# Swapping the rope halves with two DMAs instead of four, and the last layer norm moved from GpSimd to ScalarE

## The chip, the cores and the metric

The kernel runs on one core of a Trainium2 chip. The metric is the device time of one execution in microseconds (us), as the median over several executions. A core has TensorE (PE) for matmuls, VectorE (DVE), ScalarE (ACT) and GpSimd (POOL) for elementwise work, and SyncE (SP), which here only issues DMAs. Each engine runs its own instructions in order; engines wait for each other through semaphores.

## The reference

The reference is one decoder layer with a layer norm after each part, on x of 64 x 64 tokens with 256 columns:

```
x = layernorm(x + self_attention(x))          # 16 heads of 128, causal, ALiBi
x = layernorm(x + cross_attention(x, ctx))    # latent keys, 16 heads, q_rope and k_rope of 64
x = layernorm(x + ffn(x))                     # ternary weights, activations rounded to 8 bits
```

The change touches the rope of the cross-attention and the last layer norm:

```
def _rope(x, L):
    half = x.shape[-1] // 2
    ...
    x1, x2 = (x[..., :half], x[..., half:])
    return jnp.concatenate([x1 * cos - x2 * sin, x1 * sin + x2 * cos], axis=-1)

def _layernorm(x, axis=-1, eps=1e-05):
    m = jnp.mean(x, axis=axis, keepdims=True)
    v = jnp.var(x, axis=axis, keepdims=True)
    return (x - m) / jnp.sqrt(v + eps)
```

## The kernel before

The residual stream `X` stays on chip as 32 blocks of 128 tokens by 256 columns. Three parts follow each other: self-attention, cross-attention, feed-forward. Each engine's program is written out by hand, and each part is a software pipeline: in slot n an engine works on items n, n-1, n-3 and so on, in the order in which the code lists them. Values are often split into two bf16 halves, a high and a low part, and multiplied in three passes.

**Cross-attention loop.** 64 steps, 8 token tiles of 512 tokens times 8 pairs of heads. In step n:

- PE: scores of item n-3 (L914, L921), the rope part `ropeP` and the latent part `latP` of the queries of item n (L931), the weighted sum `oP` of item n-5 (L939), a transpose `ptP` of item n-4 (L947), the projection of item n-7 (L958).
- ACT: eight exponentials of item n-3 (L973), `pth` of n-4 (L980), two copies of `latP` into `qh` (L985), `oA` of item n-5 (L992).
- DVE: the reciprocal (L1013), `ptl` (L1018), the row maxima `ntop` (L1023), `turn` (L1027), then `qh` of item n-1 (two instructions, L1036), then the cosine product (L1041), once per eight steps the accumulation into `X` (L1048), in four of eight steps statistics of a block (L543).
- POOL: the normalisation of the probabilities (L1063), `oBl` (L1068), and `qhl`, the low part of `qh` (L1075), which waits for `qh`.
- SP: four DMAs `oB<-oA` for item n-6 (L893), then four DMAs `x_turned<-x_turn` for item n (L901).

The rope works on 128 partitions, two heads of 64 rows. DVE multiplies the rope part by sine (`turn`), SP's DMAs bring each row to the partition of its partner in the other half (`turned`), and one step later DVE adds the turned rows to the cosine product. The two halves of a head lie in 32 consecutive partitions each, so a swap takes four DMAs of 32 rows. The queue goes in order: the swap of item n is issued after the four DMAs of item n-6. `turn` and `turned` have two buffers.

**Feed-forward loop.** 32 blocks. In slot n: PE gate and up products of block n (`gP`, `uP`, L1211), the down product `dP` of block n-3 (L1219), transposes `hmP` of block n-2 (L1226). ACT: `sig` of block n (L1237), `ds` of block n-3 (L1243, from `dP`), `hqT` of block n-2 (L1248). DVE: `hs` of block n (L1298), its maximum (L1301), three small instructions (L1303 to L1306), then mean and variance of block n-3 (L1310, L1312), which wait for `X`. POOL: the add of `ds` to `X` for block n-3 (L1266), `hm` of block n (L1270), after every fourth block the roots of four blocks (L1257, L1259), and the normalisation of block n-7 (L1200). DVE normalises the last four blocks at the end, and SP stores four blocks with one DMA (L1288).

Of the kernel before, what the change touches and what calls it, by code (L numbers as in the profile page):

```python
# [11 lines left out]
P = 128  # L12
# [568 lines left out]
def cross_weights(a, sem, sb):  # L581


    x_stage = sb("x_stage", [P, 2, CC, TILE], F32)
    okv = sb("okv", [P, H * (C + 2 * KVC)], F32)
    wo = okv[:, 0:H * C].rearrange("p (h n) -> p h n", h=H)
    ukT = okv[:, H * C:H * (C + KVC)].rearrange("p (h n) -> p h n", h=H)
    uvT = okv[:, H * (C + KVC):].rearrange("p (h n) -> p h n", h=H)
    uqT = sb("uqT", [P, H, QC], F32)
    qr = sb("qr", [QC, H * R], F32)  # L590
    dqf, kvf, wkr = sb("dqf", [P, CC, QC], F32), sb("kvf", [P, CC, KVC], F32), sb("wkr", [KVC, 2 * R], F32)
    tabs = sb("tabs", [P, 3, T], F32)
# [7 lines left out]
    loads = [(keys[:, :], a["keys"], s_seg), (seg[0:T, :], a["segT"], s_seg), (seg[T:P, :], a["segT"], s_seg),  # L600
             (dqf[:, :, :], by_rows("L0_xattn_W_dq"), s_w), (kvf[:, :, :], by_rows("L0_xattn_W_kvc"), s_w),
             (wkr[:, :], a["wkr"], s_w), (tabs[:, :, :], a["rope"].rearrange("p (k t) -> p k t", k=3), s_w),
             (uqT[:, :, :], by_rows("uqT"), s_w), (ukT, by_rows("ukT"), s_w), (uvT, by_rows("uvT"), s_w),
             (wo, by_rows("L0_xattn_W_o"), s_w), (qr[:, :], a["L0_xattn_W_qr"], s_w)]
    return {"x_stage": x_stage, "s_ctx": [sem("l_ctx0"), sem("l_ctx1")], "okv": okv, "wo": wo, "ukT": ukT, "uvT": uvT, "uqT": uqT, "qr": qr, "dqf": dqf, "kvf": kvf, "wkr": wkr,
            "tabs": tabs, "mask": mask, "square": square, "s_mask": sem("l_mask"), "seg": seg, "segf": segf, "keys": keys, "loads": loads,
            "s_weights": s_w, "weights": 9 * 16, "s_seg": s_seg, "s_segf": sem("l_segf"), "s_square": sem("l_square"), "s_ffn": sem("l_ffn"), "s_abs": sem("l_abs"), "w_sums": sb("w_sums", [P, 3], F32)}
# [226 lines left out]
def cross_attention(nc, a, X, norm, next_norm, ident, late, sem, sb, part):  # L834
# [42 lines left out]
    with nc.Block() as block:  # L877
        @block.sync
        def _(sp):
            def ffn_weights(k, name):  # L880
                cols = CC * DFF
                src = a[name].rearrange("(c p) n -> p c n", p=P)
                dst = late["okv"][:, k * cols:(k + 1) * cols].rearrange("p (c n) -> p c n", n=src.shape[2])
                sp.dma_start(dst, src).then_inc(late["s_ffn"], 16)

            for n in range(N + PROJ_AT):
                m = n - PV_AT - 1
                if has(n, PV_AT + 1):
                    wait(sp, s_oe, m + 1)
                    wait(sp, s_proj, m - 1)  # L890
                    for par in range(2):
                        for i in range(2):
                            sp.dma_start(oB[i * KVC:(i + 1) * KVC, m % 2, par * HT:(par + 1) * HT],  # L893
                                         oA[par * KVC:(par + 1) * KVC, m % 2, i, :]).then_inc(s_ot[m % 2], 16)
                if has(n, 0):
                    wait(sp, s_turn, n + 1)
                    wait(sp, s_qh, n - 1)
                    half = R // 2
                    for r in range(0, P, half):
                        o = r + half if r % R == 0 else r - half  # L900
                        sp.dma_start(turned[o:o + half, n % 2, :], turn[r:r + half, n % 2, :]).then_inc(s_swap[n % 2], 16)  # L901
                if 8 <= n < 11:
                    ffn_weights(n - 8, ("wgT", "wuT", "wdT")[n - 8])

# [99 lines left out]
        def _(dve):  # L1004
# [3 lines left out]
            for n in range(N + PROJ_AT):  # L1008
# [14 lines left out]
                    nc.vector.tensor_reduce(ntop[:, :], by_token(sP[:, :]), AX, ALU.max, negate=True).then_inc(s_top, 1)  # L1023
                if has(n, 0):
                    wait(dve, s_ropeP, n + 1)
                    wait(dve, s_swap[n % 2], 64 * (n // 2))
                    nc.vector.tensor_tensor(by_token(turn[:, n % 2]), by_token(ropeP[n % 2][:, :]), tabs[:, 1, :].unsqueeze(1).to_broadcast([P, BT, T]),  # L1027
                                            ALU.mult).then_inc(s_turn, 1)
                if has(n, 1):
                    m = n - 1  # L1030
                    wait(dve, s_swap[m % 2], 64 * (m // 2 + 1))
                    wait(dve, s_cos, m + 1)
                    wait(dve, s_s, m - 2)
                    for i in range(2):
# [43 lines left out]
def feed_forward(nc, a, X, norm, eps_col, ident, late, out, sem, sb, part):  # L1078
# [105 lines left out]
        "sig", "h", "max", "sc", "inv", "dsc", "hm", "te", "ds", "y"))  # L1184
    s_stats, s_mom, s_rstd, s_normed, s_out = (sem("f_" + n) for n in ("stats", "mom", "rstd", "normed", "out"))
    GROUP = 4
    NG = NB // GROUP
    moments = sb("ln3_moments", [P, NB, 2], F32)
    rstd, power = sb("ln3_rstd", [P, NB], F32), sb("ln3_power", [P, GROUP], F32)
    s_eps, s_power = sem("f_eps"), sem("f_power")  # L1190

    def blocks(slot, lags):

        for n in range(NB + lags):
            slot(n, lambda lag: 0 <= n - lag < NB)

    def normalise(eng, i):

        x = X[:, i, :]
        return eng.tensor_scalar(x, x, moments[:, i, 0:1], rstd[:, i:i + 1], ALU.subtract, ALU.mult)  # L1200

    with nc.Block() as block:  # L1202
        @block.tensor
        def _(pe):
            def slot(n, has):
# [8 lines left out]
                if has(3):  # L1214
                    e = n - 3
                    wait(pe, s_te, e + 1)
                    wait(pe, s_ds, e - 1)
                    for f in range(FC):
                        last = nc.tensor.matmul(dP[e % 2][:, 0:C], hqT[:, e % 2, f * P:(f + 1) * P], wd[:, f, :], start=(f == 0), stop=(f == FC - 1))  # L1219
                    last.then_inc(s_dn, 1)  # L1220
# [11 lines left out]
        def _(act):  # L1232
            def slot(n, has):
                if has(0):
                    wait(act, s_g, n + 1)
                    wait(act, s_h, n - 1)
                    nc.scalar.activation(sig[:, n % 2, :], gP[:, :], ACT.Sigmoid, scale=gsc[:, n:n + 1]).then_inc(s_sig, 1)  # L1237
                if has(3):
                    e = n - 3
                    wait(act, s_dn, e + 1)  # L1240
                    wait(act, s_dsc, e + 1)
# [8 lines left out]
            blocks(slot, 3)  # L1250

        @block.gpsimd
        def _(pool):
            def roots(m):
                own = slice(m * GROUP, (m + 1) * GROUP)
                wait(pool, s_mom, (m + 1) * GROUP)
                nc.gpsimd.tensor_scalar(rstd[:, own], moments[:, own, 1], EPS, None, ALU.add).then_inc(s_eps, 1)  # L1257
                wait(pool, s_eps, m + 1)
                nc.gpsimd.tensor_tensor(rstd[:, own], rstd[:, own], power[:, :], ALU.pow).then_inc(s_rstd, 1)  # L1259

            def slot(n, has):
                if has(3):
                    e = n - 3
                    wait(pool, s_ds, e + 1)
                    x = X[:, e, :]
# [5 lines left out]
                if has(4) and (n - 4) % GROUP == GROUP - 1:  # L1271
                    roots((n - 4) // GROUP)
                if has(7) and n - 7 < NB - GROUP:
                    e = n - 7
                    wait(pool, s_rstd, e // GROUP + 1)
                    normalise(nc.gpsimd, e).then_inc(s_normed, 1)

            nc.gpsimd.memset(power[:, :], -0.5).then_inc(s_power, 1)
            pool.wait_ge(s_power, 1)
            blocks(slot, 4)  # L1280

        @block.sync
        def _(sp):
            dst = out.rearrange("(n p) c -> p n c", p=P)
            for m in range(NG):
                own = slice(m * GROUP, (m + 1) * GROUP)
                sp.wait_ge(s_normed, (m + 1) * GROUP)
                sp.dma_start(dst[:, own, :], X[:, own, :]).then_inc(s_out, 16)  # L1288
            sp.wait_ge(s_out, 16 * NG)

        @block.vector
        def _(dve):
            def slot(n, has):
# [12 lines left out]
                    nc.vector.tensor_scalar(dsc[:, n:n + 1], hsc[:, n:n + 1], wsc[:, 2:3], None, ALU.mult).then_inc(s_dsc, 1)  # L1306
                if has(3):
                    e = n - 3
                    wait(dve, s_y, e + 1)
                    nc.vector.bn_stats(stats[:, e, :], X[:, e, :]).then_inc(s_stats, 1)  # L1310
                    wait(dve, s_stats, e + 1)
                    nc.vector.bn_aggr(moments[:, e, :], stats[:, e, :]).then_inc(s_mom, 1)  # L1312

            blocks(slot, 3)
            dve.wait_ge(s_rstd, NG)
            for i in range(NB - GROUP, NB):
                normalise(nc.vector, i).then_inc(s_normed, 1)


def constants():  # L1320
# [7 lines left out]
    freq = 1.0 / 10000.0 ** (np.arange(half) / half)  # L1328
    ang = (np.arange(T)[:, None] * freq).T
    cos, sin = np.concatenate([np.cos(ang)] * 2), np.concatenate([-np.sin(ang), np.sin(ang)])  # L1330
    rope = np.concatenate([np.tile(cos * SCALE, (2, 1)), np.tile(-sin * SCALE, (2, 1)), np.concatenate([cos, sin])], axis=1)
    keys = np.tile(np.arange(T) + LOOKBACK / 2, (P, 1))
    return {"ident": np.eye(P, dtype=np.float32), "bias": bias.astype(np.float32),
# [34 lines left out]
```

## Time and profile before

| | |
|---|---|
| median of 3 executions | 1605.5 us (1603.73 to 1607.73) |
| profiled execution, whole / its span | 1607.42 us / 1605.6 us |
| mean granted clock of TensorE | 0.965 of full speed |
| busy in the span | PE 1426.0, ACT 1251.4, POOL 1226.7, DVE 1224.6 us |
| DMA issues `x_turned<-x_turn` | 256, of 64 KB each |
| DMA issues `oB<-oA` | 256, of 64 KB each |
| DMA issues `out<-X` | 8, of 512 KB each |

Times are from the start of the span. A row of the timeline has the start, the duration, the engine, the line and what is written from what, then in brackets the idle time of the engine before it and what ended it. Idle time of an engine that does not bound the kernel costs nothing. SPq is SP's DMA queue; its durations are issue times, and the time to landing is listed apart.

### The profile page before, as it was taken

Reading aid. Unit: us, or ns where it says so; the run is one execution under the profiler, and the core shown is the slowest. Engines: PE = TensorE matmul, PEld = TensorE weight load, DVE = VectorE, ACT = ScalarE, POOL = GpSimd, SP = SyncE. Lnnn points to the kernel's source line nnn. Section 1 sums busy time; section 2 is a strip of 40 time slices with the busy share of each in tenths; the row PEclk is TensorE's granted clock in tenths of the full one; section 3 lists DMA queues with packets and bytes.
Section 4 is the critical chain, followed back from the end, with each engine's and each line's share of the span. In section 5 each row is a group of like instructions: output and inputs, shape, how many; then the busy total and the mean of one; then the engine's idle time right before and its main releaser. Section 6 shows DMA issues by size and latency. Waiting matters only on the chain. (4 is left out here: it accounts for less than half of the span.)

```text
span 1605.6 us, 54080 instructions
## 1 busy us (share of the span) xinstructions
PE 1426.0 (89%) x19943; PEld 1060.9 (66%) x20146; DVE 1224.6 (76%) x2873; ACT 1251.4 (78%) x3981; POOL 1226.7 (76%) x1146
## 2 busy tenths in 40 slices
PE   5988999999999999999999987868889898846996
PEld 3666777777777777777777764435666666634664
DVE  3877777777777777777777787876777778747986
ACT  5877888888888888888888874667878888856664
POOL 5899889888888988888898864546667767711787
PEclk9999999999999999999999987999999999976998
DMA  6600000000000000000000001026334444310011
GB/s 225 184 3 16 16 3 16 16 2 16 16 15 3 16 16 2 16 16 3 16 16 2 3 2 54 27 58 171 95 93 99 96 97 101 94 28 0 14 40 53
DMA packets 59763, 70.64 MB, mean 44 GB/s; under 512 B 16464, under 2 KB 44432, under 8 KB 59504
## 3 DMA queue, kind: packets, MB, share of 16 engines
q1 hardware_dynamic: 59504, 67.18, 15.5%
q8 instruction: 163, 2.67, 0.7%
q14 instruction: 96, 0.79, 0.2%
HBM read 29.39 MB, written 4.19 MB: 21 GB/s over the span
## 5 line engine op out<-in xcount | busy, mean ns | idle before, releaser
L420 DVE SCALAR_TENSOR_TENSOR X<-projP,r,X 128x256 f32<-128x256 f32 x512 | 211.3, 476 | 3.7 <-PE projP L254 3.6
L1075 POOL TENSOR_TENSOR qhl<-qh 128x1024 bf16<-128x1024 f32 x64 | 121.2, 1893 | 108.5 <-issue 67.5
L234 PEld LDWEIGHTS svP<-W,xT 128*128 128x128 bf16 x3072 | 182.6, 98 | 30.5 <-issue 0.6
L973 ACT ACTIVATE x_probs<-xsP,x_ntop 128x64 f32<-128x64 f32 x512 | 152.5, 328 | 58.1 <-DVE x_ntop L1023 57.7
L480 POOL TENSOR_TENSOR y_sql<-y_sq 128x512 bf16<-128x512 f32 x128 | 133.0, 1039 | 80.8 <-ACT y_sq L321 80.4
L234 PE MATMUL svP<-W,xT 128*128 128x128 bf16 x3072 | 192.7, 219 | 0.0
L205 PE MATMUL qkssP<-xT,W 128*128 128x512 bf16 x641 | 161.8, 383 | 33.7 <-issue 20.3
L205 PE MATMUL kP<-xT,W 128*128 128x512 bf16 x768 | 188.8, 382 | 0.0
L254 PE MATMUL projP<-W,y 128*128 128x256 bf16 x1024 | 178.9, 277 | 3.3 <-POOL yl L480 3.2
L336 ACT ACTIVATE probs<-scores,ntop 128x64 f32<-128x64 f32 x512 | 170.4, 339 | 1.4 <-DVE ntop L410 1.4
L480 POOL TENSOR_TENSOR k_sql<-k_sq 128x512 bf16<-128x512 f32 x128 | 133.1, 1040 | 21.5 <-ACT k_sq L341 20.9
L254 PE MATMUL projP<-W,yl 128*128 128x256 bf16 x512 | 141.7, 277 | 0.0
L1036 DVE TENSOR_TENSOR qh<-xropeP,x_turned 64x512 f32<-64x512 f32 x128 | 88.3, 689 | 69.2 <-DMA x_turned<-x_turn 67.8
L515 POOL TENSOR_TENSOR ql<-q 128x512 bf16<-128x512 f32 x128 | 139.4, 1089 | 0.0
L480 POOL TENSOR_TENSOR q_sql<-q_sq 128x512 bf16<-128x512 f32 x128 | 133.0, 1039 | 6.9 <-ACT q_sq L328 6.9
L205 PEld LDWEIGHTS kP<-xT,W 128*128 128x128 bf16 x768 | 75.7, 99 | 92.5 <-issue 3.3
L518 POOL TENSOR_TENSOR vl<-v 128x512 bf16<-128x512 f32 x128 | 135.4, 1058 | 0.0
L480 POOL TENSOR_TENSOR yl<-y 128x512 bf16<-128x512 f32 x128 | 133.0, 1039 | 0.0
L450 DVE TENSOR_TENSOR ptl<-pyP,pth 128x256 bf16<-128x256 f32 x128 | 54.3, 424 | 96.8 <-ACT pth L355 96.8
L433 DVE COPY v<-svP 128x512 f32<-128x512 f32 x128 | 88.4, 691 | 42.8 <-PE svP L234 41.9
L205 PEld LDWEIGHTS qkssP<-xT,W 128*128 128x128 bf16 x768 | 65.0, 98 | 82.0 <-issue 13.0
L407 DVE SCALAR_TENSOR_TENSOR scores<-svP,r,bias 128x64 f32<-128x64 f32 x512 | 110.0, 278 | 4.5
(197 smaller groups left out, 4768.1 us busy)
## 6 DMA issues: line engine op xcount, KB each, us to landing
x_turned<-x_turn SPq DMA_DIRECT2D x256, 64.0 KB, 2.0
oB<-oA SPq DMA_DIRECT2D x256, 64.0 KB, 2.1
w_stage<-in_wqkvp SPq DMA_DIRECT2D x16, 512.0 KB, 3.3
x_stage<-in_xT SPq DMA_DIRECT2D x8, 512.0 KB, 4.1
X<-in_x SPq DMA_DIRECT2D x1, 4096.0 KB, 17.0
x_stage<-in_ctxT SPq DMA_DIRECT2D x8, 512.0 KB, 3.7
out<-X SPq DMA_DIRECT2D x8, 512.0 KB, 2.9
okv<-in_L_xattn_W_o SPq DMA_DIRECT2D x1, 2048.0 KB, 11.8
```

The lines of the kernel that those rows point to most:

```text
L205: last = nc.tensor.matmul(dst[:, :], weight(parity, u, i, c), xT[:, z, c, tok], start=(c == 0 and k == 0), stop=(c == CC - 1 and k == 2))
L234: last = nc.tensor.matmul(svP[:, b * D:(b + 1) * D], xT[:, u, c, t * TILE + b * P:t * TILE + (b + 1) * P], weight(parity, z, 2, c), start= ...
L254: last = nc.tensor.matmul(projP[:, b * C:(b + 1) * C], y_part, W[:, (j - 3) // NT % 2, z, 3 * CC * D:], start=(i == 0), stop=(i == 2))
L336: last = nc.scalar.activation(probs[:, b, :], scores[:, b, :], ACT.Exp, bias=ntop[:, b:b + 1], accum_out=total[:, b:b + 1])
L407: last = nc.vector.scalar_tensor_tensor(scores[:, b, :], svP[:, b * T:(b + 1) * T], r[:, b:b + 1], row, ALU.mult, ALU.add)
L420: last = nc.vector.scalar_tensor_tensor(acc, projP[:, b * C:(b + 1) * C], r[:, PB + b:PB + b + 1], acc, ALU.mult, ALU.add)
L433: nc.vector.tensor_copy(v[:, j % 4, :], svP[:, :]).then_inc(s_ve, 1)
L480: return nc.gpsimd.tensor_tensor(dst[:, :], src[:, :], high(src, slice(None), 0, TILE), ALU.subtract)
L515: nc.gpsimd.tensor_tensor(ql[:, j % 2, :], q[:, j % 2, :], high_of(q, j % 2), ALU.subtract).then_inc(s_ql, 1)
L518: nc.gpsimd.tensor_tensor(vl[:, j % 4, :], v[:, j % 4, :], high_of(v, j % 4), ALU.subtract).then_inc(s_vl, 1)
L973: last = nc.scalar.activation(probs[:, m % 2, b % PB, b // PB, :], sP[:, b * T:(b + 1) * T], ACT.Exp, bias=ntop[:, b:b + 1], accum_out=tot ...
L1075: nc.gpsimd.tensor_tensor(qhl[:, m % 3, :], flat, flat.bitcast(BF16)[:, 1::2], ALU.subtract).then_inc(s_ql, 1)
```

## The change

Two independent edits.

*Rope.* The columns of `W_qr` and of both parts of `wkr`, and the rows of the cosine and sine tables, are permuted on the host so that row i of the first half and row i of the second lie in neighbouring partitions, 2i and 2i+1. The partner of every row is now its neighbour. Two DMAs of 64 rows, each every second partition, swap them: even rows to odd ones and odd rows to even ones. The semaphore of a swap counts 32 instead of 64.

*Last layer norm.* In the loop, ACT normalises blocks 0 to 27, eight slots after the block entered, as `rstd * x + shift`, after `hqT`. POOL no longer normalises; it computes `shift = -mean * rstd` for each group of four with two more small instructions. The last four blocks form groups of three and one. For the last three blocks (29 to 31), DVE computes the add to `X` straight from `dP`, in place of `ds` on ACT and the add on POOL. The last stores are of three blocks and of one.

```
-                    half = R // 2
-                    for r in range(0, P, half):
-                        o = r + half if r % R == 0 else r - half
-                        sp.dma_start(turned[o:o + half, n % 2, :], turn[r:r + half, n % 2, :]).then_inc(s_swap[n % 2], 16)
+                    for h in range(2):
+                        sp.dma_start(turned[1 - h::2, n % 2, :], turn[h::2, n % 2, :]).then_inc(s_swap[n % 2], 16)
...
-                    wait(dve, s_swap[n % 2], 64 * (n // 2))
+                    wait(dve, s_swap[n % 2], 32 * (n // 2))
...
-                    wait(dve, s_swap[m % 2], 64 * (m // 2 + 1))
+                    wait(dve, s_swap[m % 2], 32 * (m // 2 + 1))
...
+    groups = [slice(i, i + GROUP) for i in range(0, NB - GROUP, GROUP)] + [slice(NB - GROUP, NB - 1), slice(NB - 1, NB)]
+    NG, MAIN, LATE = len(groups), NB - GROUP, NB - 3
...
         def _(act):
...
-                if has(3):
+                if has(3) and n - 3 < LATE:
...
+                if has(8) and n - 8 < MAIN:
+                    e = n - 8
+                    x = X[:, e, :]
+                    wait(act, s_shift, e // GROUP + 1)
+                    nc.scalar.activation(x, x, ACT.Identity, bias=shift[:, e:e + 1], scale=rstd[:, e:e + 1]).then_inc(s_by_act, 1)
...
         def _(pool):
             def roots(m):
...
+                if own.stop <= MAIN:
+                    nc.gpsimd.tensor_scalar(shift[:, own], moments[:, own, 0], -1.0, None, ALU.mult).then_inc(s_small, 1)
+                    wait(pool, s_small, 2 * m + 3)
+                    wait(pool, s_rstd, m + 1)
+                    nc.gpsimd.tensor_tensor(shift[:, own], shift[:, own], rstd[:, own], ALU.mult).then_inc(s_shift, 1)
...
-                if has(7) and n - 7 < NB - GROUP:
-                    e = n - 7
-                    wait(pool, s_rstd, e // GROUP + 1)
-                    normalise(nc.gpsimd, e).then_inc(s_normed, 1)
...
         def _(dve):
...
+                    if e >= LATE:
+                        x = X[:, e, :]
+                        wait(dve, s_dn, e + 1)
+                        wait(dve, s_dsc, e + 1)
+                        wait(dve, s_y, e)
+                        nc.vector.scalar_tensor_tensor(x, dP[e % 2][:, 0:C], dsc[:, e:e + 1], x, ALU.mult, ALU.add).then_inc(s_y, 1)
...
+    cos, sin = (t.reshape(2, half, T).transpose(1, 0, 2).reshape(R, T) for t in (cos, sin))
...
+    W_kr, pairs = np.asarray(inputs["L0_xattn_W_kr"]), np.arange(R).reshape(2, R // 2).T.reshape(R)
+    arrays["qr"] = np.asarray(inputs["L0_xattn_W_qr"]).reshape(QC, H, R)[:, :, pairs].reshape(QC, H * R)
+    arrays["wkr"] = np.concatenate([W_kr[:, pairs], W_kr[:, swap[pairs]]], axis=1)
```

## Rows read from the trace of the kernel before

**Rows 1.** Busy us by stretch: PE, PEld, DVE, ACT, POOL; clock, DMA share, GB/s.
```profile
1084.00:1394.00 310.00, 271.84 (x3209) 199.25 (x3263) 240.57 (x419) 253.06 (x1103) 216.43 (x168) 1.00 0.43 106
```

**Rows 2.** Waits of SP's queue, 1080 to 1390 us: total, times, longest.
```profile
SPq L893 <- ACT oA L992: 4.2, 8, 1.2
```

**Rows 3.** Timeline of SP's queue in the cross-attention loop.
```profile
1077.38 2.45 SPq L901 DMA_DIRECT2D x_turned<-x_turn  x4
...
1203.53 2.44 SPq L901 DMA_DIRECT2D x_turned<-x_turn  x4
1206.07 2.47 SPq L893 DMA_DIRECT2D oB<-oA  x4
...
1394.74 2.44 SPq L901 DMA_DIRECT2D x_turned<-x_turn  x4
```

**Rows 4.** The tile `x_turned`: its issues (ns), who waited for it, its landing.
```profile
L901 SPq DMA_DIRECT2D x_turned<-x_turn x256: 507/590/1821, 1050.7 to 1396.6; - x128
...
  DVE qh L1036: 67.8, 53
...
DMA to landing us min/median/max: 1.9/2.0/4.3
```

**Rows 5.** Timeline of DVE in the cross-attention loop.
```profile
1070.11 0.69 DVE L1027 TENSOR_TENSOR x_turn<-xropeP,tabs 128x512 f32<-128x512 f32 x1
...
1084.66 0.68 DVE L1027 TENSOR_TENSOR x_turn<-xropeP,tabs 128x512 f32<-128x512 f32 x1
...
1137.71 0.68 DVE L1027 TENSOR_TENSOR x_turn<-xropeP,tabs 128x512 f32<-128x512 f32 x1
...
1145.18 1.39 DVE L1036 TENSOR_TENSOR qh<-xropeP,x_turned 64x512 f32<-64x512 f32 x2 [1.81 <-DMA x_turned<-x_turn]
...
1148.93 0.68 DVE L1027 TENSOR_TENSOR x_turn<-xropeP,tabs 128x512 f32<-128x512 f32 x1
```

**Rows 6.** Timeline of PE, ACT and DVE over one step.
```profile
1200.46 0.81 PE L931 MATMUL xlatP<-qc,WQ 128*128 128x512 bf16 x3
...
1200.74 0.31 ACT L973 ACTIVATE x_probs<-xsP,x_ntop 128x64 f32<-128x64 f32 x1
...
1205.10 0.81 PE L931 MATMUL xlatP<-qc,WQ 128*128 128x512 bf16 x3
...
1205.30 0.69 DVE L1027 TENSOR_TENSOR x_turn<-xropeP,tabs 128x512 f32<-128x512 f32 x1
1205.38 0.31 ACT L973 ACTIVATE x_probs<-xsP,x_ntop 128x64 f32<-128x64 f32 x1
```

**Rows 7.** Waits in the feed-forward loop, 1500 to 1590 us.
```profile
DVE ln_stats L1310 <- POOL X L1266: 6.6, 6, 1.1
```

**Rows 8.** Timelines of POOL, ACT and DVE around one group's roots.
```profile
1514.98 0.23 POOL L1257 TENSOR_SCALAR ln_rstd<-ln_moments 128x4 f32<-128x4 f32 x1
1515.29 1.04 POOL L1259 TENSOR_TENSOR ln_rstd<-ln_rstd,ln_power 128x4 f32<-128x4 f32 x1
...
1515.83 1.11 ACT L1237 ACTIVATE sig<-gP,gsc 128x1024 f32<-128x1024 f32 x1
...
1518.96 1.28 DVE L1298 SCALAR_TENSOR_TENSOR hs<-uP,usc,sig 128x1024 f32<-128x1024 f32 x1
```

**Rows 9.** The page's costliest groups: busy us, mean ns, idle before.
```profile
L420 DVE SCALAR_TENSOR_TENSOR X<-projP,r,X 128x256 f32<-128x256 f32 x512 | 211.3, 476 | 3.7 <-PE projP L254 3.6
```

**Rows 10.** Groups by line, 1410 to 1486 us, before the feed-forward loop.
```profile
L1117 ACT ACTIVATE xs<-X,magic,xinv 128x256 f32<-128x256 f32 x32 | 16.6, 588 | 5.3 <-DVE xinv L1145 5.3
```

**Rows 11.** Timeline of the tail, all engines.
```profile
1594.77 1.05 PE L1219 MATMUL dP<-wd,hqT 128*128 128x256 bf16 x8 [1.12 <-ACT hqT L1248]
...
1598.38 0.43 DVE L1310 BATCH_NORM_STATS2 ln_stats<-X 128x6 f32<-128x256 f32 x1 [1.25 <-POOL X L1266]
...
1600.91 1.38 DVE L1200 TENSOR_SCALAR X<-X,ln_moments,ln_rstd 128x256 f32<-128x256 f32 x4 [1.88 <-POOL ln_rstd L1259]
```

**Rows 12.** The line of the stores: durations of the issues (ns).
```profile
L1288 SPq DMA_DIRECT2D out<-X x8: 372/372/389, 1512.6 to 1602.3; - x8
```

More of the change, by code:

```diff
@@ L603, in cross_weights @@
              (uqT[:, :, :], by_rows("uqT"), s_w), (ukT, by_rows("ukT"), s_w), (uvT, by_rows("uvT"), s_w),
-             (wo, by_rows("L0_xattn_W_o"), s_w), (qr[:, :], a["L0_xattn_W_qr"], s_w)]
+             (wo, by_rows("L0_xattn_W_o"), s_w), (qr[:, :], a["qr"], s_w)]
     return {"x_stage": x_stage, "s_ctx": [sem("l_ctx0"), sem("l_ctx1")], "okv": okv, "wo": wo, "ukT": ukT, "uvT": uvT, "uqT": uqT, "qr": qr, "dqf": dqf, "kvf": kvf, "wkr": wkr,
@@ L1186, in feed_forward @@
     GROUP = 4
-    NG = NB // GROUP
+    groups = [slice(i, i + GROUP) for i in range(0, NB - GROUP, GROUP)] + [slice(NB - GROUP, NB - 1), slice(NB - 1, NB)]
+    NG, MAIN, LATE = len(groups), NB - GROUP, NB - 3
     moments = sb("ln3_moments", [P, NB, 2], F32)
-    rstd, power = sb("ln3_rstd", [P, NB], F32), sb("ln3_power", [P, GROUP], F32)
-    s_eps, s_power = sem("f_eps"), sem("f_power")
+    rstd, shift, power = sb("ln3_rstd", [P, NB], F32), sb("ln3_shift", [P, NB], F32), sb("ln3_power", [P, GROUP], F32)
+    s_small, s_shift = sem("f_small"), sem("f_shift")
+    s_by_act = sem("f_byact")
     def blocks(slot, lags):
@@ L1195, in blocks @@
             slot(n, lambda lag: 0 <= n - lag < NB)
-    def normalise(eng, i):
-        x = X[:, i, :]
-        return eng.tensor_scalar(x, x, moments[:, i, 0:1], rstd[:, i:i + 1], ALU.subtract, ALU.mult)
     with nc.Block() as block:
@@ L1216, in slot @@
                     wait(pe, s_te, e + 1)
-                    wait(pe, s_ds, e - 1)
+                    wait(pe, s_ds, min(e - 1, LATE))
+                    wait(pe, s_y, e - 1 if e - 2 >= LATE else 0)
                     for f in range(FC):
@@ L1248, in slot @@
                     nc.scalar.activation(hqT[:, e % 2, :], tP[:, :], ACT.Copy, bias=-MAGIC).then_inc(s_te, 1)
-            blocks(slot, 3)
+                if has(8) and n - 8 < MAIN:
[3 more added lines that the diff above has]
+                    nc.scalar.activation(x, x, ACT.Identity, bias=shift[:, e:e + 1], scale=rstd[:, e:e + 1]).then_inc(s_by_act, 1)
+            blocks(slot, 4)
         @block.gpsimd
@@ L1254, in roots @@
             def roots(m):
[L1255 to L1259, printed above, removed]
+                own = groups[m]
+                wait(pool, s_mom, own.stop)
+                nc.gpsimd.tensor_scalar(rstd[:, own], moments[:, own, 1], EPS, None, ALU.add).then_inc(s_small, 1)
+                wait(pool, s_small, 2 * m + 2 - max(0, m - MAIN // GROUP))
+                nc.gpsimd.tensor_tensor(rstd[:, own], rstd[:, own], power[:, 0:own.stop - own.start], ALU.pow).then_inc(s_rstd, 1)
+                if own.stop <= MAIN:
[3 more added lines that the diff above has]
+                    nc.gpsimd.tensor_tensor(shift[:, own], shift[:, own], rstd[:, own], ALU.mult).then_inc(s_shift, 1)
             def slot(n, has):
-                if has(3):
+                if has(3) and n - 3 < LATE:
                     e = n - 3
@@ L1270, in slot @@
                     nc.gpsimd.tensor_scalar(hm[:, n % 2, :], hs[:, n % 2, :], hinv[:, n:n + 1], MAGIC, ALU.mult, ALU.add).then_inc(s_hm, 1)
-                if has(4) and (n - 4) % GROUP == GROUP - 1:
-                    roots((n - 4) // GROUP)
-                if has(7) and n - 7 < NB - GROUP:
-                    e = n - 7
-                    wait(pool, s_rstd, e // GROUP + 1)
-                    normalise(nc.gpsimd, e).then_inc(s_normed, 1)
-            nc.gpsimd.memset(power[:, :], -0.5).then_inc(s_power, 1)
-            pool.wait_ge(s_power, 1)
+                for m in range(NG):
+                    if n - 4 == groups[m].stop - 1:
+                        roots(m)
+            nc.gpsimd.memset(power[:, :], -0.5).then_inc(s_small, 1)
+            pool.wait_ge(s_small, 1)
             blocks(slot, 4)
@@ L1284, in _ @@
             dst = out.rearrange("(n p) c -> p n c", p=P)
-            for m in range(NG):
-                own = slice(m * GROUP, (m + 1) * GROUP)
-                sp.wait_ge(s_normed, (m + 1) * GROUP)
+            for own in groups:
+                if own.stop <= MAIN:
+                    sp.wait_ge(s_by_act, own.stop)
+                else:
+                    sp.wait_ge(s_normed, own.stop - MAIN)
                 sp.dma_start(dst[:, own, :], X[:, own, :]).then_inc(s_out, 16)
@@ L1314, in _ @@
             blocks(slot, 3)
-            dve.wait_ge(s_rstd, NG)
-            for i in range(NB - GROUP, NB):
-                normalise(nc.vector, i).then_inc(s_normed, 1)
+            for m in (NG - 2, NG - 1):
+                own = groups[m]
+                dve.wait_ge(s_rstd, m + 1)
+                for i in range(own.start, own.stop):
+                    x = X[:, i, :]
+                    nc.vector.tensor_scalar(x, x, moments[:, i, 0:1], rstd[:, i:i + 1], ALU.subtract, ALU.mult).then_inc(s_normed, 1)
 def constants():
@@ L1351 @@
     for name in ("L0_attn_q_rms_w", "L0_attn_k_rms_w",
-                 "L0_attn_subln_w", "L0_xattn_W_dq", "L0_xattn_W_kvc", "L0_xattn_W_o", "L0_xattn_W_qr"):
+                 "L0_attn_subln_w", "L0_xattn_W_dq", "L0_xattn_W_kvc", "L0_xattn_W_o"):
         arrays[name] = np.asarray(inputs[name])
     swap = np.concatenate([np.arange(R // 2, R), np.arange(R // 2)])
-    W_kr = np.asarray(inputs["L0_xattn_W_kr"])
-    arrays["wkr"] = np.concatenate([W_kr, W_kr[:, swap]], axis=1)
+    W_kr, pairs = np.asarray(inputs["L0_xattn_W_kr"]), np.arange(R).reshape(2, R // 2).T.reshape(R)
+    arrays["qr"] = np.asarray(inputs["L0_xattn_W_qr"]).reshape(QC, H, R)[:, :, pairs].reshape(QC, H * R)
+    arrays["wkr"] = np.concatenate([W_kr[:, pairs], W_kr[:, swap[pairs]]], axis=1)
     for short, name in (("uqT", "L0_xattn_W_uq"), ("ukT", "L0_xattn_W_uk"), ("uvT", "L0_xattn_W_uv"),
```

## The prediction, made before the changed kernel ran

> **What bounds the kernel now.** I read the page first, then busy time by stretches. The change touches two stretches: the cross-attention loop (from about 1050 us to 1426 us) and the feed-forward loop with the tail behind it (1484 us to the end). In the full part of the cross-attention loop no compute engine is busy all the time: of 310 us PE is busy 272, ACT 253, DVE 241, POOL 216, at a granted clock of 1.00 [rows 1]. Busy shares name no bound here, so I read who waits.
>
> DVE waits most: 67.8 us in 53 of 64 steps, at `qh` (L1036), for the turned rows [rows 4]. A DMA can be late because it moves slowly or because it is issued late. The queue's own waits settle that: over 310 us SP waited only 4.2 us for ACT and next to nothing for anything else [rows 2]. SP is the saturated engine. Its timeline shows the pattern: four issues of `x_turned` in 2.44 us, 0.1 us, four of `oB` in 2.47 us [rows 3], then the same gap again. That is 5.1 us a step, and some issues take longer (up to 1.8 us against a median of 0.59 [rows 4]). From step 6 to step 63 there are 57 steps between 1077.38 and 1394.74 us [rows 3], 5.57 us each.
>
> How a saturated SP becomes a lost step: `turn` ended at 1137.71 + 0.68 = 1138.39, and DVE could start the `qh` that uses it at 1145.18 [rows 5], 6.8 us later. From the start of `qh` to the end of the next-but-one `turn` DVE needs its chain of work, 1145.18 to 1149.61, 4.4 us [rows 5]. The two together are two steps, so the step is (6.8 + 4.4) / 2 = 5.6 us. This agrees with 5.57.
>
> In the feed-forward loop every fourth step has a hole: DVE waits for POOL's `X` add, six times, 1.1 us each [rows 7], because POOL computes the roots (0.23 and 1.04 us [rows 8]) before it.
>
> **The change part by part.**
>
> *Swap, issues.* Per step, two of eight issues go. The new issue has 64 rows of 2 KB, where the trace has 32 rows of 2 KB (0.59 us [rows 4]) and 64 rows of 1 KB (`oB`, a quarter of 2.47 us [rows 3]). A store of 512 KB is issued in 0.37 us [rows 12]. Neither more rows nor more bytes cost issue time there, so I take 0.61 us. SP then needs 5.1 - 1.2 = 3.9 us a step, and 0.3 to 0.4 for the long issues: 4.2 to 4.3 us. It has time over as long as the others need more, which they do (next). Bounds: 0.59 us, or 1.2 us if an issue costs by bytes; the latter makes it a rival.
>
> *Swap, landing.* The last issue of `x_turned` lands 2.0 us after it starts, with 64 KB [rows 4]. For 128 KB the bounds are 2.0 and the slowest of these, 4.3; I take 2.2, near the median, since DMA is at 0.43 of its engines' time [rows 1] and total bytes stay the same. The Trainium skill (SBUF — State Buffer, Door 1: The DMA port swizzle) says that 64 consecutive rows reach no more DMA ports than 32, while rows of both halves reach all; by it every second row of 128 has as many rows per port as the old transfer of 32, and the landing would be 2.0. No row of this trace shows ports; the sum would be some 0.1 us a step lower.
>
> *What the step becomes.* SP is free when ACT ends `oA`, which in the pattern is about 0.6 us before `turn` ends (ACT starts the next exponentials at 1205.38, `turn` ends at 1205.98 [rows 6]). It issues `oB` (2.5), then the swap: its second issue starts 1.9 + 0.1 + 0.6 = 2.6 us after `turn`, and lands 4.8 us after it; with a share of the long issues 5.1. The cycle gives (5.1 + 4.4) / 2 = 4.75 us, instead of 5.6. Other bounds: PE repeats `xlatP` from 1200.46 to 1205.10, in a step without a real hole, 4.64 us; ACT repeats its exponentials from 1200.74 to 1205.38, also 4.64 [rows 6]. ACT and PE are both full then, and DVE's accumulation (once in eight steps) can't be hidden any more: some 0.1 us per step on average. I take 4.87 us: a little above each of 4.64 and 4.75, since three tight chains disturb each other. Three steps of this very loop, before SP has built up its backlog, agree: `turn` from 1070.11 to 1084.66 [rows 5], 4.85 us each. Gain: 57 x (5.57 - 4.87) = 40 us. Bounds: 4.70 (PE's pace with the accumulations) gives 50; 5.15, halfway back to the present step, gives 24. POOL's three instructions of a step all queue behind `qh`, as its low part comes first; POOL was busy 216 of 310 us, 3.9 us a step, so it hides; where it doesn't, that is the 5.15 case.
>
> *Tables and weights permuted.* `qr`, `wkr`, cos and sin are interleaved on the host; sizes, loads and matmuls are the same: 0 us. The semaphore counts 32 instead of 64: 0 us.
>
> *Feed-forward loop.* POOL loses 28 normalisations (1.2 us each) and gains two small instructions per group. ACT gets the normalisations: the nearest row is ACT's 128x256 Identity with bias and scale, 16.6 us busy for 32 of them, 0.52 each [rows 10]. ACT's three instructions of a step leave room for it: `sig` is 1.11 [rows 8], the other two no longer, in a step of over 3.5 us, so three of four steps hide it. The fourth does not. ACT reaches the first normalisation of a group at 1515.83, where `sig` starts now [rows 8]. It waits for `shift`: POOL ends the power at 1516.33, then two small instructions. One like the 0.23 us row is fair for the first; the second is a tensor_tensor, between 0.23 and the 1.04 of the power [rows 8]; I take 0.25, as the power is what costs in that row. So `shift` is there at about 1516.9, the normalisation is out at 1517.45, and `sig` (1.11) ends at 1518.56. Queued behind it are `sig`, and DVE's `hs` behind that. `hs` starts at 1518.6 where it started at 1518.96 and could start at 1517.86 without a hole. So a hole of 1.1 us becomes one of 0.75: 6 x 0.35 = 2 us gained. With 1.04 for the product it would be 0.45 us worse each, 3 us lost; with the smallest figures 2.5 us gained.
>
> *Tail.* Now the last `dP` starts at 1594.77 and ends at 1595.82, and then POOL finishes normalisations before each add; DVE takes the last statistics at 1598.38 and starts four normalisations at 1600.91, to 1602.29 [rows 11]. After: DVE adds straight from PSUM (0.48 us by the same form in the first stage [rows 9]), to 1596.35; statistics to normalisation is 2.53 us, less 0.45 in which POOL was still normalising: 1598.4; one block, a quarter of 1.38: 1598.8. That is 3.5 us earlier. The last store is one block instead of four; the present one takes 3.3 us to the end at 1605.6; I take 0.6 less, between nothing and the 1.3 by which 3.3 exceeds the 2.0 us of a 64 KB transfer [rows 4]. Together 4.1 us, bounds 3 and 5.
>
> *Sum.* 40 + 2 + 4 = 46 us. The profiled execution took 1607.4 us, 1.8 around its span of 1605.6, and is 1.9 above the median of 1605.5. So 1607.4 - 46 = 1561.4 for that execution, 1559.5 for the median; I say 1560.
>
> **The rivals.**
>
> *A. Other waits keep the step at 5.15 us.* For it: POOL's `oBl` already ends just before PE wants it, and ACT has no slack. Against it: these waits follow `qh`. Gain 24 + 6: 1576 us.
>
> *B. PE's pace is reached.* 4.70 us: 50 + 6: 1549 us.
>
> *C. The two issues cost as much as four*, 1.2 us each: SP stays full and the step at 5.57; only the second part is left, 1600 us. For it: bytes per issue double. Against it: the store of 512 KB issued in 0.37 us [rows 12]; but it goes to another memory and all 128 rows are in order, so it is not the same thing. The Trainium skill (DMA: Bandwidth & Descriptors, Issuing engines are not separate DMA queues) holds that issue time is usually small beside the DMA; by it, saving issues would bring next to nothing and this result, too. Here the queue is hardly ever idle [rows 2, 3], and the issue time is what DVE waits for.
>
> *D. Slower: the rows a step apart run on few DMA engines.* The loop moves about 106 GB/s with 0.43 of 16 engines [rows 1], so one moves 15 GB/s. 128 KB over two engines take 4.4 us, and the landing is some 6.2 instead of 2.0. Then `turn` to `qh` is 2.6 + 6.2 = 8.8 us, the step (8.8 + 4.4) / 2 = 6.6 us, and 57 x 1.03 = 59 us are lost against 6 gained: 1658 us. It decides where landing passes 4.1 us (2.6 + 4.1 + 4.4 = two steps of 5.57), so about four engines. For it there is only that no access with a step between rows stands in the trace; against it, that the same bytes in the same row length are moved by all of them now, and that no other transfer of the loop shows such a pace.
>
> **How the numbers follow.** The forecast as summed (1550 to 1572) has 0.62, A 0.15, B 0.12, C 0.05, D 0.05, 0.01 for the rest. Leaving out D, C and a bit on the low side, the range is 1545 to 1583. A measurement of this kernel can't tell less than 0.3% (5 us) from no change. Faster: all but C and D, and half of C, as 1600 is only just past that bound: 0.92. Same 0.03, slower 0.05.
>
> **What would show it.** SP's idle time in the loop rises from 4 us to some 30 or more; two issues of `x_turned` take about 1.2 us; `turn` starts repeat every 4.9 us; DVE's wait at `qh` falls from 68 us to under 20, and PE and ACT take over as the ones without holes. In the feed-forward loop DVE's wait for `X` shrinks and a wait of `hs` for `sig` appears, 0.75 us, six times; ACT waits 1.1 us per group for `shift`. The last normalisation ends 3 us after the last `dP`, not 6.5. Wrong would be: a landing over 3 us for `x_turned`; issues near 1.2 us; a step above 5.2 with SP idle (then something in POOL or ACT is the new bound).

## The result, and the profile after

The changed kernel takes 1569.3 us (median of 4, 1564.98 to 1570.61) against 1606.6 us (median of 4) before: a ratio of 0.9765, 95% interval 0.974 to 0.979, 2.3% faster. The profiled execution has a span of 1568.8 us against 1605.6, so 36.8 us less. The forecast was 1560 us with a range of 1545 to 1583.

The 36.8 us come from three places, read from the starts of the same instructions in both traces. `turn` of step 63 starts 32.1 us earlier than before, of which 29.5 us were gained between step 6 and step 63 (57 steps of 5.07 us; before, the starts of `turn` were 5.59 us apart, and the queue's issues 5.57 [rows 3]). The feed-forward loop gives 2.1 us, the tail 4.3 us. That is 1.7 us too much; they are lost again between the last `turn` and the first `hs` (80.7 us, where it was 79.0), which the change doesn't touch.

Busy time of the full part of the cross-attention loop, columns as in [rows 1]:

```profile
1084.00:1350.00 266.00, 252.32 (x3096) 189.88 (x3094) 234.00 (x399) 240.26 (x1047) 204.26 (x157) 0.99 0.40 117
```

PE is busy 95% of it, where it was 88%; ACT 90%, where it was 82%. The waits of SP's queue, 1080 to 1360 us, answer to [rows 2]:

```profile
SPq L893 <- ACT oA L990: 48.9, 47, 2.1
SPq L42 <- PE xprojP L956: 6.0, 9, 1.7
SPq L899 <- DVE x_turn L1025: 1.0, 2, 0.5
```

The queue was hardly ever free before (4.2 us); now it waits 56 us, 49 of them for ACT's `oA`. It is no longer full. The timeline of the queue shows a step: `oB`, the swap in 1.18 us instead of 2.44, then an idle 0.86 us until the next `oB`:

```profile
1205.92 2.40 SPq L893 DMA_DIRECT2D oB<-oA  x4
1208.41 1.18 SPq L899 DMA_DIRECT2D x_turned<-x_turn  x2
1210.45 2.70 SPq L893 DMA_DIRECT2D oB<-oA  x4
```

The tile `x_turned`, which answers to [rows 4] (issue durations in ns, who waited, landing):

```profile
L899 SPq DMA_DIRECT2D x_turned<-x_turn x128: 464/590/1397, 1050.3 to 1363.7; - x128
...
  DVE qh L1034: 18.3, 16
...
DMA to landing us min/median/max: 2.0/2.1/5.4
```

An issue of twice the bytes takes the same 590 ns, it lands 0.1 us later, and DVE waits 18.3 us in 16 steps instead of 67.8 in 53. The timeline of DVE, after [rows 5]:

```profile
1072.59 0.69 DVE L1025 TENSOR_TENSOR x_turn<-xropeP,tabs 128x512 f32<-128x512 f32 x1
...
1092.02 0.69 DVE L1025 TENSOR_TENSOR x_turn<-xropeP,tabs 128x512 f32<-128x512 f32 x1
...
1100.55 0.69 DVE L1025 TENSOR_TENSOR x_turn<-xropeP,tabs 128x512 f32<-128x512 f32 x1
...
1150.76 0.69 DVE L1025 TENSOR_TENSOR x_turn<-xropeP,tabs 128x512 f32<-128x512 f32 x1
...
1155.41 0.69 DVE L1025 TENSOR_TENSOR x_turn<-xropeP,tabs 128x512 f32<-128x512 f32 x1
...
1210.40 0.69 DVE L1025 TENSOR_TENSOR x_turn<-xropeP,tabs 128x512 f32<-128x512 f32 x1
1212.44 0.69 DVE L1034 TENSOR_TENSOR qh<-xropeP,x_turned 64x512 f32<-64x512 f32 x1 [1.35 <-DMA x_turned<-x_turn]
...
1361.54 0.68 DVE L1025 TENSOR_TENSOR x_turn<-xropeP,tabs 128x512 f32<-128x512 f32 x1
```

Most steps, 38 of the 57, take 4.5 to 4.8 us, 4.67 on average, about the pace of PE and ACT in [rows 6]; the 4.65 us from 1150.76 are one. In about one of four the swap is late, by 0.5 to 2.4 us (1.35 in the row shown), and most of these steps take 5.5 to 6.5 us. The longest, 8.53 us from 1092.02, is such a one, beside the loads of the feed-forward weights. The step with the accumulation, one in eight, is about 0.85 us longer in any case. The mean is 5.07.

In the feed-forward loop (waits from 1450 to 1560 us) DVE's 6.6 us of [rows 7] have become two smaller waits (2.1 and 1.9), and ACT's wait for `shift` is new:

```profile
ACT X L1249 <- POOL ln_shift L1265: 5.9, 6, 1.0
...
DVE ln_stats L1321 <- POOL X L1272: 2.1, 6, 0.4
DVE hs L1303 <- ACT sig L1233: 1.9, 6, 0.3
```

One group, which answers to [rows 8]. `ACT X` is the new normalisation:

```profile
1486.06 0.20 POOL L1265 TENSOR_TENSOR ln_shift<-ln_shift,ln_rstd 128x4 f32<-128x4 f32 x1
...
1486.30 0.60 ACT L1249 ACTIVATE X<-X,ln_shift,ln_rstd 128x256 f32<-128x256 f32 x1 [1.05 <-POOL ln_shift L1265]
1486.81 1.10 ACT L1233 ACTIVATE sig<-gP,gsc 128x1024 f32<-128x1024 f32 x1
...
1487.93 1.28 DVE L1303 SCALAR_TENSOR_TENSOR hs<-uP,usc,sig 128x1024 f32<-128x1024 f32 x1 [0.32 <-ACT sig L1233]
```

The ACT row of L1249 waits 1.05 us for `shift` (L1265), with `sig` queued behind it. The `hs` before this one started at 1483.58, 4.35 us earlier; the step without a hole is 3.51, so the hole is 0.84 us. Before, it was 4.70 - 3.51 = 1.19. The tail, after [rows 11]:

```profile
1562.30 1.05 PE L1215 MATMUL dP<-wd,hqT 128*128 128x256 bf16 x8 [1.11 <-ACT hqT L1244]
1563.39 0.48 DVE L1319 SCALAR_TENSOR_TENSOR X<-dP,dsc,X 128x256 f32<-128x256 f32 x1 [1.88 <-PE dP L1215]
...
1565.02 0.57 POOL L1260 TENSOR_TENSOR ln_rstd<-ln_rstd,ln_power 128x1 f32<-128x1 f32 x1
```

From the start of the last `dP` to the end of the span it is 6.5 us, where it was 10.8.

### The profile page after: what moved, and what is told of

The parts are those of the page before. It is cut to its first block and busy times, and to the rows that moved or that the text cites. A ratio compares the mean times of both kernels' runs of the same rounds, so it can differ in the third digit from the quotient of the medians.

```text
span 1568.8 us, 54176 instructions
## 1 busy us (share of the span) xinstructions
PE 1441.5 (92%) x20146; PEld 1059.8 (68%) x20146; DVE 1234.5 (79%) x2876; ACT 1264.4 (81%) x4006; POOL 1195.8 (76%) x1131
## 3 DMA queue, kind: packets, MB, share of 16 engines
q8 instruction: 163, 2.67, 0.7%
## 5 line engine op out<-in xcount | busy, mean ns | idle before, releaser
L205 PE MATMUL qkssP<-xT,W 128*128 128x512 bf16 x768 | 189.6, 383 | 13.9 <-POOL W L485 11.4
L971 ACT ACTIVATION_READ_ACCUMULATOR x_probs<-xsP,x_ntop 128x1 f32 x512 | 113.2, 222 | 0.0
```

What stands on the lines that cost most here:

```text
L205: last = nc.tensor.matmul(dst[:, :], weight(parity, u, i, c), xT[:, z, c, tok], start=(c == 0 and k == 0), stop=(c == CC - 1 and k == 2))
L971: last = nc.scalar.activation(probs[:, m % 2, b % PB, b // PB, :], sP[:, b * T:(b + 1) * T], ACT.Exp, bias=ntop[:, b:b + 1], accum_out=tot ...
```

## The experiments

Each ratio is to the kernel before, timed beside it on the same chip, with its 95% interval; the changed kernel's is 0.9765 (0.974 to 0.979).

### One part at a time

The swap alone (`feed_forward` as before) and the layer norm alone (the cross-attention as before).

> The changed rope swap alone, with the feed-forward part of before. If the swap carries the gain as in the trace of the changed kernel (57 steps of 5.05 us instead of 5.57), this kernel is some 30 us faster than before, ratio 0.981, and some 6 us slower than the whole change. If the two parts interact, it is not.

> The changed last layer norm alone, with the four swap DMAs of before. From the traces: six holes of 1.19 us become 0.84 us, 2.1 us, and the tail after the last down product shrinks from 10.8 to 6.5 us: about 6.4 us faster than before, ratio 0.996. The rival, that the tail's gain is only the time in which the stores of the faster kernel were already out, gives under 3 us.

Measured: the swap alone 1574.2 us, 0.9796 (0.9780 to 0.9813), 33 us less. The layer norm alone 1601.2 us, 0.9963 (0.9951 to 0.9976), 5.9 us less. The two sum to 2.4% against 2.35% for both: they add. The trace of the first has 5.04 us per step, that of the second the same three waits as above (5.8, 2.1 and 1.9 us).

In the code below `...` stands for the rest of an edit, such as the counts of semaphores.

### The number of issues, or the new pattern?

```
-                    for h in range(2):
-                        sp.dma_start(turned[1 - h::2, n % 2, :], turn[h::2, n % 2, :]).then_inc(s_swap[n % 2], 16)
+                    for r in range(0, P, R):
+                        for h in range(2):
+                            sp.dma_start(turned[r + 1 - h:r + R:2, n % 2, :], turn[r + h:r + R:2, n % 2, :]).then_inc(s_swap[n % 2], 16)
...
```

> The changed kernel with the same interleaved halves, but four DMAs of 32 rows each per step instead of two of 64. Theory: what counts is the number of issues on SP. Then the step goes back to 5.5 to 5.6 us, the queue is never idle, and the kernel is some 30 us slower than the changed one (ratio to before 0.995). Rival: the gain came from moving every second row, which lands or shares DMA engines better. Then it stays near the changed kernel, ratio 0.977.

Measured: 1599.5 us, 0.9959 (0.9942 to 0.9976), so only the second part's gain is left. The steps are 5.58 us long. The waits of SP's queue (1080 to 1350 us) and two turns of its timeline:

```profile
SPq L893 <- ACT oA L991: 0.7, 2, 0.5
```

```profile
1204.01 2.45 SPq L900 DMA_DIRECT2D x_turned<-x_turn  x4
1206.56 2.46 SPq L893 DMA_DIRECT2D oB<-oA  x4
1209.12 3.08 SPq L900 DMA_DIRECT2D x_turned<-x_turn  x4
```

The queue is full again, with every second row moved. The gain is the number of issues and not the pattern.

The converse: two issues, but of consecutive rows (the rope then gets wrong partners).

```
-                        sp.dma_start(turned[1 - h::2, n % 2, :], turn[h::2, n % 2, :]).then_inc(s_swap[n % 2], 16)
+                        sp.dma_start(turned[64 - 64 * h:128 - 64 * h, n % 2, :], turn[64 * h:64 * h + 64, n % 2, :]).then_inc(s_swap[n % 2], 16)
```

> The changed kernel, but its two swap DMAs move 64 consecutive rows each (rows 0 to 63 to 64 to 127 and back), so the rope is fed with the wrong partners; issues and bytes are the same. If only the number of issues counts, the landing stays at 2.1 us and the time within 3 us of the changed kernel (ratio 0.977). By the Trainium skill (SBUF — State Buffer, Door 1: The DMA port swizzle) 64 consecutive rows reach half of the ports that every second row of 128 reaches, so the landing would be longer, by an estimate of 0.2 to 0.3 us from the bytes, and with it the step by 0.1 us, some 6 us in all.

Measured: 1568.1 us, 0.9757 (0.9737 to 0.9777), the same as the changed kernel. The landing of its `x_turned`:

```profile
DMA to landing us min/median/max: 2.2/2.4/6.6
```

It is 2.4 us against 2.1 for every second row, with equal bytes and rows. By the rule of the Trainium skill (SBUF — State Buffer, Door 1: The DMA port swizzle), 64 consecutive rows reach half of the ports that every second row of 128 reaches. These two landings agree with it: 0.3 us more for 64 rows in one block. That did not reach the time: the step is 5.08 us against 5.07, where 6 us in all had been worked out from the rule. From 1080 to 1350 us DVE waits more often (24 times against 14) and 4 us longer in total (21.8 us against 17.8), and the loop is only 0.7 us longer. So short waits are absorbed in part.

### What is left of the step

The pace of PE and ACT is 4.64 us, the step 5.07. Two suspects: late swaps, and DVE's accumulation once in eight steps. First, SP freed of two `oB` issues a step (half of `oB` stays zero, so half of the weighted sum is missing):

```
-                        for i in range(2):
+                        for i in (par,):
                             sp.dma_start(oB[i * KVC:(i + 1) * KVC, m % 2, par * HT:(par + 1) * HT],
...
```

> The changed kernel with two of the four oB DMAs of each step left out (half of oB stays zero, so half of the weighted sum is missing). SP then issues four instead of six DMAs a step, and the swap is issued 1.2 us earlier after turn. Theory: the rest of the loss over the pace of 4.64 us is partly late swaps (18 us of DVE waits): these waits fall under 5 us and the step falls from 5.05 to about 4.8 us, some 12 us. Rival: SP is no bound any more and the step is set by the accumulation and by PE and ACT; then it stays at 5.0 us, within 3 us.

Measured: 1548.0 us, 0.9638 (0.9622 to 0.9654), 20 us less than the changed kernel, more than the 12 expected. The wait at `qh` (1080 to 1350 us) and DVE's timeline:

```profile
DVE qh L1036 <- DMA x_turned<-x_turn: 2.3, 3, 1.1
```

```profile
1200.69 0.69 DVE L1027 TENSOR_TENSOR x_turn<-xropeP,tabs 128x512 f32<-128x512 f32 x1
1205.33 0.69 DVE L1027 TENSOR_TENSOR x_turn<-xropeP,tabs 128x512 f32<-128x512 f32 x1
1209.97 0.69 DVE L1027 TENSOR_TENSOR x_turn<-xropeP,tabs 128x512 f32<-128x512 f32 x1
1214.61 0.69 DVE L1027 TENSOR_TENSOR x_turn<-xropeP,tabs 128x512 f32<-128x512 f32 x1
```

Here the steps average 4.64 us but for the one with the accumulation, which is 5.49 (and a few of 4.9 to 5.5, most of them near the weight loads); the mean is 4.78. Next, the accumulation cut to 32 of 1024 columns (the rest of the result is left out):

```
-                        acc = X[:, tile * PB:(tile + 1) * PB, :]
+                        acc = X[:, tile * PB:(tile + 1) * PB, 0:8]
...
```

> The changed kernel with the accumulation into X cut from 1024 to 32 columns per tile (the rest of the cross-attention's result is left out). Theory: the accumulation costs one step in eight 0.85 us and upsets the swap after it; eight of them are 7 us, so 1562 us. Rival: it is hidden, and time is unchanged within 2 us.

Measured: 1559.6 us, 0.9715 (0.9691 to 0.9738), some 8 us less, about the 7 expected. Steps are 4.96 us, and DVE's wait for the swap stays (18.2 us from 1080 to 1340 us, against 17.8). So the residue of 0.43 us per step divides into about 0.1 for the accumulation (5.07 - 4.96) and 0.3 for late swaps.

### Mending the late swaps

In the changed kernel the swap is issued behind the four `oB`. The obvious edit is to turn them round (this version ran after the one below, to which its expectation refers):

```
+                if has(n, 0):
+                    wait(sp, s_turn, n + 1)
+                    wait(sp, s_qh, n - 1)
+                    for h in range(2):
+                        sp.dma_start(turned[1 - h::2, n % 2, :], turn[h::2, n % 2, :]).then_inc(s_swap[n % 2], 16)
                 m = n - PV_AT - 1
                 if has(n, PV_AT + 1):
...
```

> The changed kernel with nothing but SP's order turned: swap first, then the four oB. The swap is then in time, but oB lands about 1.8 us later, and in the changed kernel POOL's low part of it ends just before PE's projection wants it. Theory: late swaps are traded for late projections, PE waits 0.8 us per step at the projection, step 5.3 us or more: slower than the changed kernel by 10 us or more. Rival: oB has room, and the order alone gives the gain of e6: 1554 us.

Measured: 1593.4 us, 0.9907 (0.9878 to 0.9936): by the ratios 23 us slower than the changed kernel, steps of 5.55 us. The waits, 1080 to 1340 us:

```profile
POOL oBl L1066 <- DMA oB<-oA: 48.0, 34, 3.3
...
PE xprojP L956 <- POOL oBl L1066: 37.6, 29, 2.4
```

DVE hardly waits for the swap any more (2.2 us), but POOL waits for `oB` and PE for POOL. Now the same edit, with room made for `oB`: the projection one step later (and before the weighted sum on PE), and on POOL the low part of `qh` one step later and before that of `oB`.

```
-    S_AT, T_AT, PV_AT, PROJ_AT = 3, 4, 5, 7
+    S_AT, T_AT, PV_AT, OL_AT, PROJ_AT = 3, 4, 5, 7, 8
...
-                if has(n, 1):
-                    m = n - 1
+                if has(n, 2):
+                    m = n - 2
                     wait(pool, s_lat, m + 1)
...
```

> The changed kernel with SP issuing the swap before the four oB DMAs of a step, and room made for the later oB: the projection one step later (item n-8) and before the weighted sum on PE, and on POOL the low part of qh one step later and before that of oB. The swap then starts right after turn and has 1.9 us to spare. Theory that late swaps (queued behind oB, or hit by a slow DMA) cost the step 0.27 us: DVE's wait at qh goes under 3 us, steps are 4.64 us except for the accumulation's, mean 4.78, and the time is 1552 to 1556 us. Rival that e4 was fast because of less DMA traffic and fewer bytes, not because of the order: no more than 5 us faster than the changed kernel.

Measured: 1553.7 us, 0.9669 (0.9651 to 0.9687), 15 to 16 us faster than the changed kernel, as expected. All DMAs and bytes are those of the changed kernel, so half as many `oB` transfers are not needed for the gain: steps are 4.79 us, as with half of `oB` (4.78). A part comes from the new order on PE and POOL: the step with the accumulation takes 5.28 us instead of 5.49, 1.5 us in seven of them. The new order without the earlier swap was not run. DVE's wait for the swap (1080 to 1340 us) is 6.7 us, not the under 3 expected:

```profile
DVE qh L1034 <- DMA x_turned<-x_turn: 6.7, 3, 3.0
```

All three fall after the loads of the feed-forward weights. DVE's timeline there has steps of 7.14 and 6.38 us, and one of 5.56 behind them:

```profile
1090.86 0.69 DVE L1025 TENSOR_TENSOR x_turn<-xropeP,tabs 128x512 f32<-128x512 f32 x1
1098.00 0.68 DVE L1025 TENSOR_TENSOR x_turn<-xropeP,tabs 128x512 f32<-128x512 f32 x1
1104.38 0.68 DVE L1025 TENSOR_TENSOR x_turn<-xropeP,tabs 128x512 f32<-128x512 f32 x1
```

### The hole in the feed-forward loop

```
+                for m in range(NG):
+                    if n - 4 == groups[m].stop - 1:
+                        roots(m)
                 if has(0):
                     wait(pool, s_inv, n + 1)
...
-                for m in range(NG):
-                    if n - 4 == groups[m].stop - 1:
-                        roots(m)
```

> The changed kernel with POOL's roots and shift of a group between the add and hm of a step instead of after hm, where POOL sits idle for 1.7 us. Theory: the hole of 0.84 us in every fourth step comes from shift being late for the normalisation in front of sig, and from the add behind the roots. Then six holes vanish, hs repeats every 3.51 us and the kernel is 5 us faster than the changed one (ratio to before 0.9735). Rival: PE is as full as DVE, and the hole only moves to PE: under 1 us.

Measured: 1562.4 us, 0.9723 (0.9709 to 0.9737), against 0.9765: 6.7 us less, with intervals that leave room for the 5 expected. (The profiled execution is its slowest, at 1568.7 us.) From 1480 to 1512 us DVE waits for nothing, and ACT only for PE; `hs` starts every 3.51 us over nine starts (1478.75 to 1506.86), with two groups' roots among them, for instance the two starts below. In the rest of the loop, too, no step of this kernel is over 3.6 us:

```profile
1492.80 1.28 DVE L1303 SCALAR_TENSOR_TENSOR hs<-uP,usc,sig 128x1024 f32<-128x1024 f32 x1
1496.32 1.28 DVE L1303 SCALAR_TENSOR_TENSOR hs<-uP,usc,sig 128x1024 f32<-128x1024 f32 x1
```

### Together

> The reordered cross-attention loop and the earlier roots together, nothing else changed. If the two gains lie in different parts and add, as the first two experiments did, the time is 1553.7 less 5 to 7: 1547 to 1549 us, ratio to before 0.963.

Measured: 1549.6 us, 0.9645 (0.9621 to 0.9668). That is 4 to 5 us less than the reordered loop alone (by the ratios or the medians), a little short of the 5 to 7 expected but within the intervals. The starts of `hs` are 3.5 to 3.6 us apart throughout, so the holes are gone here, too. The steps of the cross-attention loop are 4.81 us, against 4.79. The last edit splits the loads of the weights:

```
-                if 8 <= n < 11:
-                    ffn_weights(n - 8, ("wgT", "wuT", "wdT")[n - 8])
+                if 8 <= n < 20:
+                    k = (n - 8) // 4
+                    ffn_weights(k, ("wgT", "wuT", "wdT")[k], (n - 8) % 4)
...
```

> The same, with the feed-forward weights fetched in twelve DMAs of 256 KB over twelve steps instead of three of 1 MB over three steps. Theory: the three slow steps after the loads (7.1, 6.4 and 5.6 us in the reordered kernel against 4.63) come from swaps that share the DMA engines with a load of 1 MB; split, they cost 1 to 2 us in all instead of 5: 1543 to 1545 us. Rival: the same bytes take the same time from the swaps wherever they are, and the time does not change.

Measured: 1545.6 us, 0.9611 (0.9589 to 0.9633), the fastest version, 3.9% below the kernel before and 24 us below the changed one. Against the 1543 to 1545 expected it is half a microsecond over. The slowest landing of a swap, first without and then with the split:

```profile
DMA to landing us min/median/max: 1.9/2.1/8.3
...
DMA to landing us min/median/max: 1.9/2.1/4.6
```

The seven steps around the loads take 36.0 us instead of 38.4, so they cost 2.9 us over the usual steps where it was 5.4 (expected: 1 to 2 instead of 5). The mean step is 4.77 us against 4.81. So the bytes of the weights cost less in pieces of 256 KB, and the rival, no change, is out for this stretch. But the loop as a whole is only 2.2 us shorter. The profiled executions differ by 3.5 us, and 2.1 us of that lie before the loop, where the two kernels are the same. The ratios' intervals overlap a little, but each execution with the split (1543.7 to 1546.1 us) is faster than the fastest without (1548.1). So the gain is real, and some 2 of its 4 us are shown to come from the split; where the rest comes from is open.

## Why the prediction was right

**The bound.** The prediction named SP's issue time as the bound of the loop, from a queue that waited 4 us of 310. The experiments with four strided issues and with two consecutive ones show it: at equal bytes, time follows the number of issues, whichever rows they move. Rivals C and D (an issue costs by bytes; rows a step apart run on few engines) are out: 590 ns an issue, 2.1 us a landing, for the 0.61 and 2.2 taken.

**The step.** This is the term that was mis-sized: 57 x (5.57 - 4.87) = 40 us was forecast, 29.5 us was measured, which is 57 times the difference of 5.59 and 5.07. The bounds were sound, the pace of 4.64 us and about 0.1 for the accumulation: freed of nearly all late swaps, the loop ran at 4.78 us, and at 4.77 in the best version. What failed is the way in which the late swaps entered. The prediction put "a share of the long issues", 0.3 us, on the time from `turn` to `qh`, found (5.1 + 4.4) / 2 = 4.75, which is hardly over 4.64, and so took lateness as nearly hidden. But lateness does not come in equal shares. Three swaps of four are in time; the fourth is late, by 1.3 us on average from 1080 to 1350 us, and where it is over a microsecond late, DVE's next row maxima and ACT's exponentials shift by nearly all of it. PE and ACT, with little slack of their own, don't win it back. 18.3 us of waits in 57 steps are 0.32 us a step; with 0.1 for the accumulation this gives 4.64 + 0.43 = 5.07. The three early steps of 4.85 us, which seemed to confirm the sum, were too few: they were 5.12, 4.50 and 4.93 us long.

**The feed-forward loop.** A hole of 0.75 us was forecast, and 0.84 was measured; 6 x 0.35 = 2.1 us was right: the old hole was 0.09 us larger than taken, too (1.19 for 1.1), so that the two errors cancelled, which is luck. It was made as described, ACT waiting 1.05 us for `shift` with `sig` behind it. A part of it, 0.36 us, is still DVE's wait for the add behind the roots; it overlaps with the lateness of `sig`, so `hs` itself shows a wait of only 0.32. The product with `rstd` takes 0.20 us for the 0.25 taken.

**The tail.** 4.1 us forecast, 4.3 measured. From the start of the last `dP`, the last normalisation ends 3.8 us earlier than before (3.5 taken), and the store behind it saves 0.5 (0.6 taken). The layer norm alone gave 5.9 us for the 6.1 of both terms.

**The size of the whole.** 46 us forecast, 37 measured; the step alone makes the difference. Rival A had the nearer step, 5.15 us, and the nearer time: 1569 us lies 9 us above the forecast and 7 below A's 1576. But A had it for another reason, waits in POOL and ACT. So the bound was right and the loop's gain was taken a third too large; the range held because it had room for A.

## What to carry to other kernels

A DMA queue that almost never waits is a bound like an engine: count its issues per step and compare with the step, and choose a data layout in which one transfer does the work of two. (Issuing a part of the transfers from another engine was not tried here.) Where the chains behind a transfer have no slack, its occasional lateness costs nearly in full, so cost it event by event and not as a mean inside a maximum (short delays may be absorbed, long ones were not); then give it slack by issuing it first, and only after the transfer that it displaces has been given a step more. Small work of one engine that others wait for belongs where that engine sits idle: moving POOL's roots by one position took away the whole hole.

## What the runs showed of the hardware

- Issue time does not follow rows or bytes between these: 590 ns for 32 rows or 64 rows of 2 KB, a step of two between rows included; 0.6 us for 64 rows of 1 KB; 372 ns for a store of 512 KB to the output, in the trace of before.
- Every second of 128 rows lands after 2.1 us, 64 consecutive rows after 2.4, at 128 KB each.
- Late swaps coincide with transfers of instructions. The page lists 163 of them in one queue (2.67 MB, so 16 KB each, 0.7% of 16 engines' span, about 1.1 us each). In the changed kernel's loop one comes every 10.7 us, in 28 of the 57 steps. DVE waits for the swap of 15 of these 28 steps, and of the other 29 for one, by 0.2 us. The kernel with the new swap alone shows the same: 17 of 28, and 2 of 29 (0.2 and 0.5 us). Of the 15, seven swaps landed after 3.3 to 3.9 us, seven were late by long issues (mostly the four `oB` before the swap, 2.7 to 3.8 us instead of 2.4), and one landed beside the weight loads, after up to 5.4 us. Where a swap was 1.35 us late, at 1212.44, one such transfer lies in the stretch from 1207 to 1213 us, and the two swap DMAs landed after 2.5 and 3.4 us instead of 2.1:

```profile
q8 instruction: 1, 0.02, 1.4%
```

```profile
DMA to landing us min/median/max: 2.5/2.9/3.4
```

  In other cases an issue of SP itself is long, as in the four `oB` that took 3.79 us at 1251.10 instead of 2.4, again with one such transfer beside it. With the swap issued first the transfers are still there, every 10 us, but the only waits left are those at the weight loads. That the instruction transfer is the cause was not tested: no kernel here changed the amount of instructions alone. It is a strong coincidence, seen in both forms.
